# A hybrid conv and Fourier-mixer kernel: 25-point products, inverse and half of the mix in 64 by 64 parts of the array

## The chip, the cores and the metric

The kernel runs on one core of one Trainium2 chip. The time is that of the device in microseconds, from the first instruction to the last. A core has TensorE (a 128 by 128 array for matmuls, which writes PSUM), VectorE, ScalarE, GpSimd and SyncE (which here issues the DMAs). Each engine works through its own list of instructions in order and waits on semaphores for the others.

## The reference, cut to what matters

```python
B, R, C, H = 64, 55, 96, 192                      # 64 images, 55 x 55, 96 channels; 3025 tokens each
# layer 0: depthwise 25 x 25 convolution with every third tap, gate, residual
x = conv(x, raw_kernel * mask) * x + bias + x
# layer 1, t = tokens of x
h = relu(bn(layernorm(t) @ w1.T))                 # 3025 x 192
X = fft(h, axis=tokens, norm='ortho')
rd, idg = diagonal(r), diagonal(i)
xr = relu(X.real * rd - X.imag * idg + rb)
xi = relu(X.imag * rd + X.real * idg + ib)
y = ifft(xr + 1j * xi, axis=tokens, norm='ortho').real
t = t + bn(y @ w2.T)                              # back to 96 channels
t = t + ffn(layernorm(t))                         # 96 -> 384 -> 96, relu, inputs rounded to fp8
```

## The kernel before

It has two stages, one after the other: the convolution for all images (up to about 860 us), and the mixer for all images. Only the mixer is touched.

The mixer does the Fourier transform of 3025 = 121 x 25 points in two steps. First a product over the 121 rows (`rows`, 128 outputs: real and imaginary part of 62 row frequencies k1, in order [real/imaginary, kk, p] with k1 = 2p + kk). Its result goes to DRAM (`a_d`) and comes back (`acol`) with the 25 tokens on the partitions: 100 partitions are real/imaginary and kk times 25. Then, for each of 31 pairs p of row frequencies, the 25-point product with twiddles (`columns`, constants `fb`, 100 by 100). What is computed there for two values of kk does not mix, so half of each 100 by 100 constant is zero. The outputs have channels on the partitions, 96 at a time (`hf` is the half of the 192 channels), and stand in two PSUM banks (`COL`). The gate makes xr and xi of it: `gate_value` and the three operations of `gate_sum` on ScalarE, `value` (two operations), `larger` and `join` on VectorE, `cut_value` and `add_sum` on GpSimd. Then `mix` multiplies by w2 (two matmuls for each pair, one for each half of the channels, which accumulate), `out_mix` copies, `inverse` is the inverse 25-point product (100 by 100 again), `out_inverse` copies, the result goes through DRAM (`g_d`) into `grow`, and `inverse_rows` ends the transform. The feed-forward part follows: `normalise`, `turn2`, `up`, `out_up`, `widen_bias`, `down`, `out_down`, `finish`.

Everything is a software pipeline over 512 chunks, eight per image. In slot g of the schedule each engine runs one chunk of every stage, each at its own distance behind: GATE = 10 means that columns, gate_value and gate_sum of chunk g - 10 stand in slot g; MIX is 14, INV 15, ROWS 29, UP 41, DOWN 42. A chunk of the token stages is three tokens (of 25), the first of the eight is four. A chunk of the frequency stages is 8 pairs (7 in the last group) for one half of the channels; mix and inverse take four pairs (three in the last). The order within a slot is written out by hand, once for each engine: the four loops `for g in SLOTS_G` at the end of the engines' blocks. Buffers are few: most PSUM banks have one use per slot, so nearly every matmul group waits until the copy of the group before it in the same bank is done.

The lines that matter: the products L1033, widen L1045 (copy with relu L811), rows L1058 (copy L864), mix L1073 and L1074 (copy L819), inverse L1085 (copy L825), down L1097 (copy L833), turn L1110 (copy L841), up L1123 (copy L850), inverse rows L1134, turn2 L1145 (copy L780); the gate on ScalarE L789, L798, L801, L803. The second half of a chunk's rows is done in the next slot, `rows(g - 1, 1)`. The waits that the prediction follows: rows wait for relu of their own half, up for out_down of the chunk before (which stands in the same slot), mix for out_up of the slot before:

```python
            def rows(n, part):
                pe.wait_ge(hid_ready, 2 * n + part + 1)
            def up(n):
                pe.wait_ge(z_ready, n)
            def mix(n):
                    pe.wait_ge(y16_ready, upto(n + MIX - UP))
```

Of the kernel before, what the change touches and what calls it, by code (L numbers as in the profile page):

```python
# [84 lines left out]
SLOTS = PAIRS_K + 1  # L85
M = 4 * SLOTS
# [4 lines left out]
MIXED = (0, 4, 8, 12, 16, 20, 24, 28, 31)  # L91
# [30 lines left out]
def pairs_of(n):  # L122
    return MIXED[n % NS], MIXED[n % NS + 1]

# [6 lines left out]
def here(n):  # L131
    return 0 <= n < CHUNKS
# [6 lines left out]
def transform_constants():  # L139
# [15 lines left out]
    for kk in range(2):  # L155
        for p in range(PAIRS_K):
# [8 lines left out]
    out = {"c_fa": fa, "c_fb": fb.reshape(Q, PAIRS_K, Q), "c_ib": ib.reshape(Q, PAIRS_K, Q),  # L165
           "c_ia": np.ascontiguousarray(fa.T), "c_id": np.eye(128)}
# [180 lines left out]
def mixer_stage(nc, x1, p, a_d, g_d, out):  # L347
    with ExitStack() as ctx:
# [8 lines left out]
        fb = sb("fb", [Q, PAIRS_K, Q])  # L357
        ib = sb("ib", [Q, PAIRS_K, Q])
# [3 lines left out]
        w2t = sb("w2t", [HH + 1, 2, C])  # L362
        rd = sb("rd", [HH, 2])
        nrd = sb("nrd", [HH, 2])
        idg = sb("idg", [HH, 2])
        rb = sb("rb", [HH, 2])
        ibias = sb("ibias", [HH, 2])
# [11 lines left out]
        acol = sb("acol", [Q, PAIRS_K, H])  # L379
        spec = sb("spec", [HH + 1, 2, PAIRS_K, Q])  # L380
        gc = [sb(f"gc{s}", [HH, KC, Q // 2]) for s in range(2)]
        gq = [sb(f"gq{s}", [HH, KC, Q // 2]) for s in range(2)]
        gv = [sb(f"gv{s}", [HH, KC, Q // 2]) for s in range(2)]
        mixed = sb("mixed", [Q, SLOTS, C])
# [21 lines left out]
        with ExitStack() as wctx:  # L406
            def wsem(name):
# [4 lines left out]
            w2n = t_res[0:C, 2:4, :].rearrange("p a b -> p (a b)")  # L412
# [11 lines left out]
            rows = [spec[C:C + 1, 1, 2 * n:2 * n + 2, 0:C] for n in range(4)]  # L424
            rows2 = [spec[C:C + 1, 1, 8 + n, 0:C] for n in range(4)]
# [3 lines left out]
                      [spec[C:C + 1, 1, 12 + 2 * n:14 + 2 * n, 0:C] for n in range(2)],  # L429
                      [spec[C:C + 1, 1, 16 + n, 0:C] for n in range(2)]]  # L430
# [9 lines left out]
            LOADS = 30  # L440
# [3 lines left out]
            def _(sp):  # L444
# [4 lines left out]
                ld(ib[:, :, :], p["c_ib"])  # L449
# [3 lines left out]
                ld(w2n, p["w2"])  # L453
# [12 lines left out]
                ld(rb[:, :], p["rb"].rearrange("(a p) -> p a", a=2))  # L466
                ld(ibias[:, :], p["ib"].rearrange("(a p) -> p a", a=2))
                for dst, k in ((rd, "r"), (idg, "i")):
                    flat = p[k].rearrange("a b -> (a b)")
                    for a in range(2):  # L470
                        at = a * HH * (H + 1)
                        ld(dst[:, a:a + 1],
                           flat[at:at + (HH - 1) * (H + 1) + 1:H + 1].rearrange("(p o) -> p o", o=1))
# [739 lines left out]
```

## Time and profile before

| | us |
|---|---|
| median of 3 runs | 5028.19 |
| their range | 5025.69 to 5029.70 |
| the profiled execution | 5025.73 |
| its span in the trace | 5023.9 |
| mean granted TensorE clock | 0.964 |

Busy shares in the profile are times in which an engine had an instruction under way. A TensorE row with "x16" is 16 passes merged: it begins with the first start and ends with the last end. The ends of passes are modelled, and passes overlap, so what a stretch of passes costs is read from start to start. An f32 matmul shows as two passes, each with a weight load (PEld) of its own. Shapes of TensorE rows read: contraction rows * output partitions, then the moving operand. In the timeline the first number is the start in us, the second the duration, and brackets give the idle time just before and the instruction that ended it. The granted clock is a share of 2.4 GHz.

The page's slices:

```profile
PE   8999995599999999999999999999999999999964
DVE  3444443347888888888888888888888888888885
ACT  3444442278888888888888888888888888888853
PEclk9999997599999999999999999999999999999985
```

Each digit is a fortieth of the span, in tenths. The convolution is in the first seven, then comes the set-up of the mixer, and from the ninth on the mixer runs evenly until the last two.

### The profile page before, as it was taken

How to read it: one execution, taken by the hardware profiler on the slowest of the kernel's cores; microseconds unless marked ns; L12 is line 12 of the kernel's file. 1: busy time of each engine (PE TensorE's matmuls, PEld its weight loads, DVE VectorE, ACT ScalarE, POOL GpSimd, SP SyncE). 2: the span in 40 equal slices, each digit the busy share in tenths (PEclk: the TensorE clock that was granted, in tenths of full speed). 3: DMA queues.
4: the chain of work that ended last, by engine and by line, in shares of the span. 5: the costliest groups of instructions: out<-in, count | busy, mean ns of one | idle time of the engine just before them, and what ended most of it. 6: DMA issues, size and time to landing. Idle time of an engine off the chain costs nothing.

```text
span 5023.9 us, 121831 instructions
## 1 busy us (share of the span) xinstructions
PE 4688.8 (93%) x40863; PEld 4162.2 (83%) x40863; DVE 3875.6 (77%) x10873; ACT 3777.1 (75%) x7819; POOL 2493.3 (50%) x2603
## 2 busy tenths in 40 slices
PE   8999995599999999999999999999999999999964
PEld 7888884388888888888888888888888888888852
DVE  3444443347888888888888888888888888888885
ACT  3444442278888888888888888888888888888853
POOL 2334432144555555555555555555555555555542
PEclk9999997599999999999999999999999999999985
DMA  6777876256666666666666666666666666666541
GB/s 202 244 232 226 250 230 179 77 146 183 176 181 182 182 180 176 176 180 180 181 179 179 176 179 182 179 182 178 181 183 174 178 180 180 180 179 178 160 112 32
DMA packets 781424, 893.16 MB, mean 178 GB/s; under 512 B 236243, under 2 KB 689292, under 8 KB 768652
## 3 DMA queue, kind: packets, MB, share of 16 engines
q1 hardware_dynamic: 780556, 885.27, 63.9%
q8 instruction: 347, 5.69, 0.5%
q14 instruction: 257, 2.11, 0.1%
q10 hardware_dynamic: 264, 0.10, 0.0%
HBM read 500.64 MB, written 384.61 MB: 176 GB/s over the span
## 4 chain that ended last, share of the span: by engine, by line
PE 64%; DVE 13%; issue 3%; ACT 2%; DMA 0%; DVEq 0%; POOL 0%; POOLq 0%; ACTq 0%
PE ps L1033 10%; PE ps L1058 10%; PE ps L1045 9%; PE ps L1085 6%; PE ps L1074 6%; PE ps L1073 6%; PE ps L1134 5%; PE ps L1123 4%; PE ps L1097 4%; PE ps L1110 3%; DVE y L933 1%; PE ps L1145 1%; DVE bn L988 1%; DVE gv L958 1%; DVE xn L973 1%
## 5 line engine op out<-in xcount | busy, mean ns | idle before, releaser
L733 POOL TENSOR_SCALAR gv<-gv 96x400 f32<-96x400 f32 (+1 forms) x512 | 599.8, 1171 | 1615.4 <-DVE xn L973 1529.9
L1033 PE MATMUL ps<-fb,acol 100*96 100x100 f32 x7936 | 785.0, 252 | 44.0 <-DVE spec L965 43.6
L340 PE MATMUL cps<-toep,xin 114*128 114x190 f32 (+2 forms) x3456 | 777.2, 339 | 44.5 <-issue 25.4
L850 ACT ACTIVATE y<-ps 128x1089 f16<-128x1089 f32 (+1 forms) x512 | 573.0, 1119 | 315.9 <-PE ps L1123 315.9
L1058 PE MATMUL ps<-hid,fa 121*128 121x384 f32 (+1 forms) x2048 | 729.7, 438 | 46.7 <-DVE t L997 34.4
L1033 PEld LDWEIGHTS ps<-fb,acol 100*96 100x96 f32 x7936 | 722.1, 163 | 61.2 <-issue 60.8
L317 DVE SCALAR_TENSOR_TENSOR xo<-cps,xo 128x180 f32<-128x180 f32 (+3 forms) x576 | 362.8, 630 | 460.9 <-ACT xo L286 460.5
L286 ACT ACTIVATE xo<-cps 128x180 f32<-128x180 f32 (+3 forms) x576 | 367.4, 638 | 452.7 <-PE cps L343 452.7
L1045 PE MATMUL ps<-w1t,xnt 97*121 97x192 f32 x3200 | 701.2, 330 | 0.7 <-ACT xnt L841 0.7
L1073 PE MATMUL ps<-w2t,spec 97*100 97x96 f32 x3968 | 672.9, 251 | 4.7 <-ACT y L850 4.7
L1074 PE MATMUL ps<-w2t,spec 96*100 96x96 f32 x3968 | 675.6, 252 | 0.0
L933 DVE TENSOR_SCALAR y<-y,b1q 128x364 f16<-128x364 f16 (+1 forms) x1536 | 572.6, 427 | 98.7 <-ACT y L850 98.2
L340 PEld LDWEIGHTS cps<-toep,xin 114*128 114x128 f32 x3456 | 531.7, 194 | 108.8 <-issue 31.1
L295 POOL TENSOR_TENSOR xo<-xo,conv_cbias 128x3960 f32<-128x3960 f32 (+1 forms) x39 | 317.6, 8169 | 516.3 <-DVE xo L317 516.3
L939 DVE CAST hq<-y 128x1092 fp8e5<-128x1092 f16 (+1 forms) x512 | 517.5, 1011 | 53.8 <-DVE y L933 1.4
L1073 PEld LDWEIGHTS ps<-w2t,spec 97*100 97x100 f32 x3968 | 546.3, 167 | 5.2 <-POOL spec L739 2.7
L1085 PEld LDWEIGHTS ps<-mixed,ib 100*100 100x100 f32 x3968 | 430.8, 168 | 144.4 <-issue 78.5
L1045 PEld LDWEIGHTS ps<-w1t,xnt 97*121 97x121 f32 x3200 | 525.1, 187 | 19.0 <-issue 1.2
L1074 PEld LDWEIGHTS ps<-w2t,spec 96*100 96x100 f32 x3968 | 510.3, 168 | 0.0
L811 ACT ACTIVATE hid<-ps 121x384 f32<-121x384 f32 (+1 forms) x1024 | 432.7, 423 | 92.7 <-PE ps L1045 53.9
L739 POOL TENSOR_TENSOR spec<-spec,gc 96x400 f32<-96x400 f32 (+1 forms) x512 | 484.8, 947 | 0.0
L864 ACT ACTIVATE arow<-ps 128x384 f32<-128x384 f32 (+1 forms) x1024 | 426.5, 417 | 57.4 <-PE ps L1058 55.5
(107 smaller groups left out, 10243.1 us busy)
## 6 DMA issues: line engine op xcount, KB each, us to landing
a_d<-arow SPq DMA_DIRECT2D x448, 288.0 KB, 5.0
acol<-a_d SPq DMA_DIRECT2D x192, 600.0 KB
xin<-in_items SPq DMA_DIRECT2D x96, 1008.0 KB
g_d<-mixed SPq DMA_DIRECT2D x256, 300.0 KB
tok<-x_d SPq DMA_DIRECT2D x64, 1134.4 KB
out<-o_sb SPq DMA_DIRECT2D x448, 136.1 KB
x_d<-xo SPq DMA_DIRECT2D x48, 990.0 KB, 11.9
grow<-g_d SPq DMA_DIRECT2D x128, 312.0 KB, 11.1
```

The costliest lines, as they stand in the source:

```text
L340: last = nc.tensor.matmul(ps[2 * (m % DEEP)][:, (r0 - o0) * GC:(r1 - o0) * GC], xb, toep[e % 2][0:GP, c, at * GC:(at + r1 - r0) * GC], sta ...
L733: nc.gpsimd.tensor_scalar(v, v, 0.0, None, ALU.max).then_inc(v_cut, 1)
L739: nc.gpsimd.tensor_tensor(sv, sv, gc[t % 2][:, 0:n, :], ALU.add).then_inc(s_ready, 1)
L850: nc.scalar.activation(y16[n % 2][:, :, 0:w], ps[:, MIXP:MIXP + FM, 0:w], ACT.Copy).then_inc(y16_ready, 1)
L933: last = nc.vector.tensor_scalar(y[:, m, 0:w], y[:, m, 0:w], b1q[:, m:m + 1], 0.0, ALU.add, ALU.max)
L939: nc.vector.tensor_copy(q[:, :, 0:w], y[:, :, 0:w], saturate=False).then_inc(hq_ready, 1)
L1033: last = nc.tensor.matmul(COL[:, p, 0:Q], acol[:, p0 + p, hf * HH:(hf + 1) * HH], fb[:, p0 + p, :], start=True, stop=True)
L1045: last = nc.tensor.matmul(ps[0:U, WIDE, j * H:(j + 1) * H], xnt[n % 2][:, s0 - c0 + j, :], w1t[:, :], start=True, stop=True)
L1058: nc.tensor.matmul(ps[0:M, ROW, 0:(s1 - s0) * H], fa[:, :], hid[part][:, 0:s1 - s0, :].rearrange("p j h -> p (j h)"), start=True, stop=Tru ...
L1073: nc.tensor.matmul(o, spec[0:HH + 1, 0, p, :], w2t[0:HH + 1, 0, :], start=True, stop=False)
L1074: last = nc.tensor.matmul(o, spec[0:HH, 1, p, :], w2t[0:HH, 1, :], start=False, stop=True)
L1085: last = nc.tensor.matmul(ps[0:Q, INVP, (p - p0) * C:(p - p0 + 1) * C], ib[:, p, :], mixed[:, p, :], start=True, stop=True)
```

## The change

K2 is 50, HALF 64, S 25, C 96, QG 8. The constants, their tiles and the gate's tiles take another shape, the products, the inverse and half of the mix become matmuls with at most 64 rows and 64 columns, and the order within a slot changes on TensorE, ScalarE and VectorE.

- `columns`: the zero half of each constant is dropped. kk (now r) has the partitions 64r to 64r + 49 of `acol` and `fb`, and its 50 by 50 products go to bank r. The channels are cut in 128 and 64 instead of 96 and 96. In a slot with hf = 0 there are 8 pairs x 2 r x 2 blocks of 64 channels = 32 matmuls, in one with hf = 1 16, whose outputs alternate between the lower and the upper 64 partitions. Each has 64 output rows and 50 columns. Consecutive matmuls go round the four quarters of the array.
- The gate works on 128 partitions: 400 elements for hf = 0, 200 for hf = 1 (before 400, or 350 in the last group, in both).
- `mix`: for the first 128 channels one whole-array matmul per tile of two row frequencies (114 output partitions), then for the last 64 channels two matmuls of 64 rows and 50 outputs each, which accumulate onto it. The bias of the second batch norm becomes a matmul of its own in the first chunk of an image (before, a row of ones in `spec`).
- `inverse`: 8 matmuls of 50 rows and 64 outputs instead of 4 of 100 by 100. Mix and inverse share two PSUM banks now, so `inverse` waits for the `out_mix` of the chunk that stands in the same slot.
- Order: on TensorE the products move behind the mix and the inverse directly behind them, ahead of rows(g, 0). On ScalarE out_mix comes behind relu(g, 0), then gate_value, the copy of rows(g, 0), out_inverse, and only then gate_sum. On VectorE value and larger move from the end of the slot to the next slot, behind residual.
- The column loads and the mixed stores are issued in two halves each. The rows of `c_ia` are in another order to match.

```diff
@@ tiles @@
-        fb = sb("fb", [Q, PAIRS_K, Q])
-        ib = sb("ib", [Q, PAIRS_K, Q])
+        fb = sb("fb", [128, SLOTS, K2])
+        ib = sb("ib", [128, 2, TILES, HALF])
-        acol = sb("acol", [Q, PAIRS_K, H])
-        spec = sb("spec", [HH + 1, 2, PAIRS_K, Q])
+        acol = sb("acol", [128, PAIRS_K, H])
+        spec = [sb("spec0", [128, 4, 2 * QG, HALF]), sb("spec1", [128, 4, QG, HALF])]
-        TURNED, WIDE, ROW, MIXP, INVP, DOWNP = 2, 3, 4, 5, 6, 7
+        TURNED, WIDE, ROW, MIXP, DOWNP = 2, 3, 4, 5, 7
@@ TensorE, columns @@
-                for p in range(n):
-                    last = nc.tensor.matmul(COL[:, p, 0:Q], acol[:, p0 + p, hf * HH:(hf + 1) * HH],
-                                            fb[:, p0 + p, :], start=True, stop=True)
+                for k in range(QG):
+                    l, j = (k, 0) if hf == 0 else (k // 4 * 4 + k % 2 * 2 + k // 2 % 2, k % 2)
...
+                    for r in range(2):
+                        for h in range(2 - hf):
+                            at = HALF * (h + j)
...
+                            last = nc.tensor.matmul(ps[at:at + HALF, r, c0:c0 + K2],
+                                                    acol[HALF * r:HALF * r + K2, p, HALF * (h + 2 * hf):HALF * (h + 2 * hf) + HALF],
+                                                    fb[HALF * r:HALF * r + K2, p, :], start=True, stop=True)
@@ TensorE, mix @@
-                for p in range(p0, p1):
-                    o = ps[0:Q, MIXP, (p - p0) * C:(p - p0 + 1) * C]
-                    nc.tensor.matmul(o, spec[0:HH + 1, 0, p, :], w2t[0:HH + 1, 0, :], start=True, stop=False)
-                    last = nc.tensor.matmul(o, spec[0:HH, 1, p, :], w2t[0:HH, 1, :], start=False, stop=True)
+                for a in range(tiles):
+                    at = (QG * r + 2 * a) * HALF
+                    nc.tensor.matmul(ps[0:HALF + K2, MIXP + a % 2, MIXC + a // 2 * C:MIXC + (a // 2 + 1) * C],
+                                     wide[:, at:at + HALF + K2], w2t[:, 0, :],
+                                     start=(a < 2), stop=False, skip_group_check=True)
...
+                for a in range(tiles):
+                    j = a % 2
+                    for b in range(2):
+                        last = nc.tensor.matmul(ps[HALF * b:HALF * b + K2, MIXP + j, MIXC + a // 2 * C:MIXC + (a // 2 + 1) * C],
+                                                spec[1][HALF * j:HALF * j + HALF, q, QG // 2 * r + a // 2 * 2 + b, 0:K2],
+                                                w2t[HALF * j:HALF * j + HALF, 1, :],
+                                                start=False, stop=True, skip_group_check=True)
@@ TensorE, inverse @@
-                pe.wait_ge(w2_ready, n + 1)
+                pe.wait_ge(w2_ready, upto(n + 2))
...
-                    last = nc.tensor.matmul(ps[0:Q, INVP, (p - p0) * C:(p - p0 + 1) * C], ib[:, p, :],
-                                            mixed[:, p, :], start=True, stop=True)
+                    for b in range(2):
+                        last = nc.tensor.matmul(ps[HALF * j:HALF * j + HALF, MIXP + b, INVC + a // 2 * C:INVC + (a // 2 + 1) * C],
+                                                ib[HALF * b:HALF * b + K2, r, 4 * q + a, :],
+                                                mixed[HALF * b:HALF * b + K2, QG * q + 4 * r + a, :],
+                                                start=True, stop=True, skip_group_check=True)
@@ VectorE, slot @@
                 if here(g - RES):
                     residual(g - RES)
+                if here(g - GATE - 1):
+                    value(g - GATE - 1)
+                    larger(g - GATE - 1)
...
-                if here(g - GATE):
-                    value(g - GATE)
-                    larger(g - GATE)
```

ScalarE, one slot of the kernel before, from gate_value (`gq`) on; `spec`, `gc` and the write to `ps` are gate_sum:

```order
L789 ACTIVATE gq1<-ps,ibias,idg 96x400
L864 ACTIVATE arow2<-ps 128x192
L811 ACTIVATE hid0<-ps 121x384
L798 ACTIVATE spec<-ps,idg 96x8x50
L801 ACTIVATE gc1<-ps,rb,rd 96x400
L803 ACTIVATE ps<-ps,rb,rd 96x8x50
L819 ACTIVATE mixed<-ps 100x384
L864 ACTIVATE arow0<-ps 128x384
L825 ACTIVATE mixed<-ps 100x384
L833 ACTIVATE z161<-ps 121x288
L841 ACTIVATE xnt0<-ps 97x484
L811 ACTIVATE hid1<-ps 121x192
```

ScalarE, the same stretch in the changed kernel; `mixed` is out_mix first and out_inverse second:

```order
L900 ACTIVATE arow0<-ps 128x192
L840 ACTIVATE hid0<-ps 121x384
L856 ACTIVATE mixed<-ps 114x2x2x96
L819 ACTIVATE gq0<-ps,ibias,idg 128x400
L900 ACTIVATE arow1<-ps 128x384
L861 ACTIVATE mixed<-ps 114x2x2x96
L827 ACTIVATE spec0<-ps,idg 128x16x25
L830 ACTIVATE gc0<-ps,rb,rd 128x400
L832 ACTIVATE ps<-ps,rb,rd 128x16x25
L869 ACTIVATE z160<-ps 121x288
L877 ACTIVATE xnt1<-ps 97x363
L840 ACTIVATE hid1<-ps 121x384
```

The gate's last three operations stood ahead of the copies of mix, rows and inverse and now stand behind them; gq follows out_mix.

TensorE, the kernel before, from rows(g, 0) of one slot to the first products of the mix in the next:

```order
L1058 MATMUL ps<-hid,fa 128x384
L1085 MATMUL ps<-mixed,ib 100x96 x4
L1097 MATMUL ps<-w2q,hq 128x96 x9
L1110 MATMUL ps<-ident,toks 97x121 x4
L1045 MATMUL ps<-w1t,xnt 121x192
L1134 MATMUL ps<-grow,ia 121x288
L1123 MATMUL ps<-xq,w1q 128x363 x3
L1145 MATMUL ps<-ident,xn 96x121 x3
L1033 MATMUL ps<-fb,acol 96x100 x7
L1058 MATMUL ps<-hid,fa 128x192
L1045 MATMUL ps<-w1t,xnt 121x192 x2
L1073 MATMUL ps<-w2t,spec 100x96
```

TensorE, the changed kernel, from rows(g - 1, 1) to turn2, one slot:

```order
L1102 MATMUL ps<-hid,fa 128x192
L1089 MATMUL ps<-w1t,xnt 121x192 x2
L1121 MATMUL ps<-w2t,spec 114x96 x4
L1130 MATMUL ps<-w2t,spec 50x96 x8
L1076 MATMUL ps<-fb,acol 64x50 x32
L1146 MATMUL ps<-mixed,ib 64x96 x8
L1102 MATMUL ps<-hid,fa 128x384
L1160 MATMUL ps<-w2q,hq 128x96 x12
L1173 MATMUL ps<-ident,toks 97x121 x3
L1089 MATMUL ps<-w1t,xnt 121x192
L1197 MATMUL ps<-grow,ia 121x288
L1186 MATMUL ps<-xq,w1q 128x363 x3
```

The products (`fb,acol`) led the slot, ahead of the rows with 192 columns; now they stand behind both kinds of mix, and the inverse (`mixed,ib`) ahead of the rows with 384 columns. The second listing has three kinds of small matmul in a row and whole ones before and after.

## Rows read from the trace of the kernel before

**Rows 1.** page, first part: busy us, share of the span and passes of each engine
```profile
PE 4688.8 (93%) x40863; PEld 4162.2 (83%) x40863; DVE 3875.6 (77%) x10873; ACT 3777.1 (75%) x7819; POOL 2493.3 (50%) x2603
```

**Rows 2.** groups of instructions, 2000 to 4000 us: line, engine, tiles, shapes, count, busy, mean
```profile
L1033 PE MATMUL ps<-fb,acol 100*96 100x100 f32 x4092 | 403.1, 251 | 14.7 <-DVE spec L965 14.7
```

**Rows 3.** timeline of TensorE, a plain slot: start us, us, line, tiles, shapes, count
```profile
3034.14 1.57 PE L1033 MATMUL ps<-fb,acol 100*96 100x100 f32 x16
3035.54 0.52 PE L1058 MATMUL ps<-hid,fa 121*128 121x192 f32 x2
3035.89 0.81 PE L1045 MATMUL ps<-w1t,xnt 97*121 97x192 f32 x4
3036.55 0.33 PE L1073 MATMUL ps<-w2t,spec 97*100 97x96 f32 x2
...
3037.95 0.84 PE L1058 MATMUL ps<-hid,fa 121*128 121x384 f32 x2
...
3040.88 0.63 PE L1123 MATMUL ps<-xq,w1q 96*128 96x363 fp8e5 x3
3041.35 0.33 PE L1145 MATMUL ps<-ident,xn 121*96 121x121 fp8e5 x3
3041.51 0.71 PE L1033 MATMUL ps<-fb,acol 100*96 100x100 f32 x6
```

**Rows 4.** timeline of ScalarE, the next slot; in brackets the idle time before
```profile
3044.50 0.58 ACT L798 ACTIVATE spec<-ps,idg 96x400 f32<-96x400 f32 x1
3044.98 0.68 ACT L801 ACTIVATE gc<-ps,rb,rd 96x400 f32<-96x400 f32 x1
3045.55 0.65 ACT L803 ACTIVATE ps<-ps,rb,rd 96x400 f32<-96x400 f32 x1
...
3046.41 0.49 ACT L864 ACTIVATE arow<-ps 128x384 f32<-128x384 f32 x1
3046.78 0.50 ACT L825 ACTIVATE mixed<-ps 100x384 f32<-100x384 f32 x1
3047.15 0.43 ACT L833 ACTIVATE z<-ps 121x288 f16<-121x288 f32 x1
3047.44 0.50 ACT L841 ACTIVATE xnt<-ps 97x363 f32<-97x363 f32 x1
3047.79 0.36 ACT L811 ACTIVATE hid<-ps 121x192 f32<-121x192 f32 x1
3048.72 1.08 ACT L850 ACTIVATE y<-ps 128x1089 f16<-128x1089 f32 x1 [0.57 <-PE ps L1123]
```

**Rows 5.** set-up: busy by stretch (granted clock third last), the line's durations, timeline
```profile
860.00:900.00 40.00, 2.18 (x31) 1.80 (x31) 19.00 (x58) 0.83 (x4) 0.00 (x0) 0.50 0.17 37
...
L575 PE MATMUL ps<-ident,stage x24: 311/311/367, 888.4 to 889.0; 64*64 64x64 f32 x24
...
887.73 0.69 PE L570 MATMUL ps<-ident,t_res 96*128 96x96 f32 x3
...
888.05 0.37 PE L570 MATMUL ps<-ident,t_res 96*128 96x96 f32 x1
888.35 0.38 PE L575 MATMUL ps<-ident,stage 64*64 64x64 f32 x4
...
888.35 0.49 PE L575 MATMUL ps<-ident,stage 64*64 64x64 f32 x8
```

**Rows 6.** timeline of TensorE while the mixer fills, rows behind a wait
```profile
995.05 0.91 PE L1058 MATMUL ps<-hid,fa 121*128 121x384 f32 x2 [0.58 <-ACT hid L811]
```

**Rows 7.** timeline of TensorE while the mixer fills, two slots on
```profile
1039.40 1.58 PE L1033 MATMUL ps<-fb,acol 100*96 100x100 f32 x16 [0.24 <-DVE spec L965]
...
1045.94 1.58 PE L1033 MATMUL ps<-fb,acol 100*96 100x100 f32 x16 [0.53 <-DVE spec L965]
```

**Rows 8.** busy time by stretch: TensorE, loads, VectorE, ScalarE, GpSimd, clock, DMA
```profile
3000.00:4000.00 1000.00, 983.96 (x9181) 885.07 (x9180) 895.33 (x2619) 874.90 (x1861) 558.55 (x660) 1.00 0.67 179
4808.00:4820.00 12.00, 8.40 (x87) 6.85 (x85) 11.45 (x33) 6.75 (x12) 6.30 (x7) 1.00 0.14 39
```

More of the change, by code:

```diff
@@ L85 @@
 SLOTS = PAIRS_K + 1
+K2 = 2 * S
+HALF = 64
+TILES = SLOTS // 2
+QG = 8
 M = 4 * SLOTS
@@ L378, in mixer_stage @@
         arow = [sb(f"arow{s}", [M, JC, H]) for s in range(AR)]
-        acol = sb("acol", [Q, PAIRS_K, H])
-        spec = sb("spec", [HH + 1, 2, PAIRS_K, Q])
[L381 to L384, printed above, removed]
+        acol = sb("acol", [128, PAIRS_K, H])
+        spec = [sb("spec0", [128, 4, 2 * QG, HALF]), sb("spec1", [128, 4, QG, HALF])]
+        gc = [sb(f"gc{s}", [128, 2 * QG, S]) for s in range(2)]
+        gq = [sb(f"gq{s}", [128, 2 * QG, S]) for s in range(2)]
+        gv = [sb(f"gv{s}", [128, 2 * QG, S]) for s in range(2)]
+        mixed = sb("mixed", [128, SLOTS, C])
         grow = sb("grow", [M, S, C])
@@ L542, in _ @@
                 nc.vector.tensor_copy(ident8[:, :], ident[0:U, 0:U], saturate=False)
-                nc.vector.memset(mixed[:, PAIRS_K, :], 0.0)
+                for v in spec:
+                    nc.vector.memset(v[:, :, :, K2:HALF], 0.0)
                 for v in toks:
@@ L549, in _ @@
                     nc.vector.memset(v[:, :, :], 0.0)
-                then(nc.vector.memset(spec[HH:HH + 1, :, :, :], 0.0))
-                nc.vector.memset(spec[HH:HH + 1, 0, 0, 0:1], 1.0)
             @block.scalar
@@ L675, in store_mixed @@
                 sp.wait_ge(g_ready, n + 1)
-                p0, p1 = GROUP[q], GROUP[q + 1] if q < 3 else SLOTS
-                sp.dma_start(g_d[i].rearrange("s (r p) c -> (s r) p c", p=SLOTS)[:, p0:p1, :],
-                             mixed[:, p0:p1, :]).then_inc(g_stored[q], 16)
+                dst = g_d[i].rearrange("s (ri j p) c -> j (s ri) p c", ri=2, j=2)
+                for j in range(2):
+                    sp.dma_start(dst[j, :, QG * q:QG * (q + 1), :],
+                                 mixed[j * HALF:j * HALF + K2, QG * q:QG * (q + 1), :]).then_inc(g_stored[q], 16)
             def load_back(i, h):
@@ L784, in gate_value @@
             def gate_value(t):
-                n, hf = group(t)[2:]
+                _, hf, n = group(t)
                 act.wait_ge(x_done, t + 1)
@@ L875, in _ @@
                     relu(g, 0)
+                if here(g - MIX):
+                    out_mix(g - MIX)
+                if here(g - GATE):
+                    gate_value(g - GATE)
+                if here(g):
+                    rows_out(g, 0)
+                if here(g - INV):
+                    out_inverse(g - INV)
                 if here(g - GATE):
@@ L948, in value @@
             def value(t):
-                p0, p1, n, hf = group(t)
-                xi = COL[:, 0:n, Q // 2:Q]
-                dv = spec[0:HH, hf, p0:p1, Q // 2:Q]
+                _, hf, n = group(t)
+                xi, dv = column(t, 1), spectrum(t, 1)
                 dve.wait_ge(c_ready, t + 1)
@@ new lines, in mix @@
+                for a in range(tiles):
[3 more added lines that the diff above has]
+                                     start=(a < 2), stop=False, skip_group_check=True)
+                if n % NS == 0:
+                    nc.tensor.matmul(ps[0:HALF + K2, MIXP, MIXC:MIXC + C], hot[:, :], wb[:, :],
+                                     start=False, stop=False, skip_group_check=True)
@@ L1157, in _ @@
                     mix(g - MIX)
+                if here(g - GATE):
+                    columns(g - GATE)
+                if here(g - INV):
+                    inverse(g - INV)
                 if here(g):
                     rows(g, 0)
-                if here(g - INV):
-                    inverse(g - INV)
                 if here(g - DOWN):
```

162 lines of the change are left out of this document (91 added, 71 removed).

## The prediction

> **What bounds the kernel now.** I began with the busy shares. TensorE is busy for 93% of the span, VectorE 77%, ScalarE 75% [rows 1]. The slices show a convolution stage up to about 860 us and then the mixer, in which nothing changes until 4840 us; the change touches only the mixer. There the mean slot of the schedule comes from the grouped view: 4092 passes of the 25-point products in 2000 us, and a batch of eight slots has 124 of them, so 33.0 batches, 60.6 us each, **7.58 us a slot** [rows 2]. The timeline of a plain slot (three tokens, 16 product passes) is 7.37 us of TensorE without a hole, from 3034.14 to 3041.51 [rows 3]. ScalarE has the same period and waits 0.57 us in it for the up-projection [rows 4]. So TensorE is the bound, and work taken from it should show, as long as no chain of waits across engines becomes longer than its work.
>
> An f32 matmul is two passes. With 96 to 100 columns on either side, loads and streams overlap and a pass costs 0.088 us: 16 products take 1.40 us (3034.14 to 3035.54), 16 of the mix 1.40 us, so 8 of the inverse 0.70 us. Two passes of rows with 192 columns take 0.35 us [rows 3]. I read from this 2 cycles a column of the wider side at 2.4 GHz and some 5 to 15 ns; a whole pass of 114 columns is then 0.10 us.
>
> **What the parts cost.** The trace has one burst of the kind that the change uses: 24 passes of 64 by 64 in the set-up, going round the four quarters. The clock is 0.50 there, 1.2 GHz [rows 5]. A merged row runs from its first start to its last end, and a pass shows 0.311 us (the first ones 0.367): four passes have begun by about 888.37, eight by 888.53, and the last of 24 begins at 889.0 [rows 5]. So behind the second group come four groups in about 0.45 us, 0.11 us each. That is one pass's own 128 cycles of 1.2 GHz, so four run at once, 27 ns a pass. At 2.4 GHz I take four per pass time of the wider side: 0.058 us for 64 columns (14.5 ns each), 0.085 us for 96 (21 ns each). This is an extrapolation; it is held at 27 ns below for the upper bound. Entering the parts is not free: the last whole pass before the burst began at 888.05 and the first small one at 888.35, where whole ones followed at 0.16 us, and the second small group ends its starts 0.16 us after the first and not 0.11: 0.19 us more in all, at half clock [rows 5]. No row has the way back at full clock. I bound a change of form by nothing and 0.3 us, and take 0.15 us, twice a slot.
>
> The Trainium skill's TensorEngine Tiling (Key Properties) says that a change of tiling mode drains TensorE. The 0.30 us gap agrees. By that rule two drains per slot are due, by a free switch none.
>
> TensorE's work per slot, before and after, in us. Products: 1.40 becomes 64 passes in a slot with the first 128 channels ("wide"), 0.93, and 32 in one with the last 64 ("narrow"), 0.46. Mix: 16 passes, 1.40, become 8 whole ones at 0.10 and 16 small ones at 0.021, 1.14. Inverse: 0.70 becomes 16 at 0.021, 0.34. With two switches: 3.50 becomes 2.71 or 2.24. TensorE alone would fall by about 1 us per slot, to some 6.5 us. ScalarE and VectorE lose something too: a narrow gate has 200 elements instead of 400, and ScalarE's copies of 288 and 384 elements (0.29 and 0.37 us) [rows 4] show 0.8 ns an element, so 0.17 us an operation, four on each.
>
> **The wait that the order makes.** The change moves the products behind the mix and, on ScalarE, the gate's three operations behind the two copies that wait for work after the products. Follow it round: rows(g-1, 1) may begin only when relu(g-1, 1) is done, the last but one thing that ScalarE does in its slot. Then TensorE does rows, widen, mix, products, inverse and rows(g, 0); ScalarE copies the result of rows(g, 0), copies the inverse, does the gate's three, out_down, out_turn and relu(g, 1); and only then the next slot's second rows can begin. Also up(g-41) waits for out_down of the same slot. Before, the same ring was some 5.4 us (0.35, 0.65, 1.40, 0.67 and 0.87 to the inverse's end, then copies and relu of 1.4 us), because the gate stood before the copy of rows(g, 0) and the products before rows(g-1, 1). Now nearly everything is in it. Clock it from the start of rows(g-1, 1), wide slot:
>
> - rows 0.35, and 0.07 since its load can't be made ahead (0.91 us behind a wait, 0.84 us without) [rows 3, 6]; widen 0.65: 1.07. The mix also waits for out_up of the slot before: that up begins 0.63 us ahead of our zero, its last pass ends 0.63 us after its start, hand-over 0.04, out_up 1.08, hand-over 0.05: 1.18. With 0.07 for the load: 1.25.
> - whole mix 0.80: 2.05. Switch 0.15, small mix 0.34: 2.54. Products 0.93: 3.47. Inverse 0.34, switch 0.15: 3.96. rows(g, 0) 0.84 to its end [rows 3]: 4.80.
> - ScalarE [rows 4]: 0.04, arow 0.37, inverse 0.37: 5.58. Gate 0.48, 0.57, 0.57: 7.20. out_down 0.43: 7.63.
> - up 0.05 later, 0.47, and 0.16 for turn2: **8.31**. The other branch (z 0.29, xnt 0.35, relu 0.36, 0.05) gives 8.25.
>
> Narrow slot: the products are done before out_mix. Small mix ends at 2.54 + 0.17 of tail, 0.04, out_mix 0.49, 0.05: 3.29; inverse 3.63; rows(g, 0) ends at 4.62; copies 5.40; gate 1.11: 6.51; out_down, up and turn2: **7.62**. The mean is 7.96. In a batch one slot has the four-token rows (0.3), one the four-token out_up (0.3), with 0.1 in small copies; the last mix has three tiles (-0.4); the root adds 0.13: together +0.06 per slot. So **8.02 us against 7.58, +0.44 us** in the 470 slots in which all stages run: +207 us. In the 28 slots of the fill that have products and mix, but no down or up, a slot takes 6.54 us now [rows 7]; the ring without out_down and up is 7.8 or 7.1: +0.9 us, +25 us. Seven more small loads and a memset in the set-up: some 5 us. Sum on the profiled execution, whose span is 5023.9 us (its own time is 5025.7, the median of the runs 5028.2): **5260 us**.
>
> Edits that I cost at nothing: VectorE's value and larger now follow residual; the products wait for them, but residual ends before rows(g-1, 1) begins and 1.65 us of work is done well before 2.54. They push the cast that down waits for back by 1.65 us; down now starts later in the slot as well. If that cover is gone, turn and widen follow late, off the ring, up to about a microsecond. The two halves of each column load and of each mixed store carry the same bytes on SP, with one more issue each, two slots ahead of use. The bias matmul (two passes a batch) is 0.2 us.
>
> **Rivals.**
> - Small passes have a floor. If no more than one pass per 27 ns can be issued also at full clock (the rate of the burst), small mix and inverse are 0.43 each and products 1.71 or 0.85: +0.96 us wide, +0.28 us narrow, +0.62 us mean: 5570 us. For it: no row shows a faster sustained rate. Against it: within a group starts are 5 to 7 ns apart, and 27 ns is just what the half clock gives. The Trainium skill's TensorE: Matmul & The Clock Gate (on the 56 ns gap) has a floor of 25 ns from start to start; the starts within the burst do not obey it, and its sustained form would give this rival.
> - Faster than before. If queued passes start as closely as within a group of the burst (6 ns) and a switch costs nothing, 64 passes cost 0.4 us and the mix's small part 0.1. The ring then falls to 7.3 and 6.8, with the extras 7.1, and the time to 5025.7 - 0.48 x 470, 4800 us. It decides once the mean slot of 8.02 falls by 0.44 us: switches (0.30) and the two exposed loads with what hangs on them (0.2) hold that much and no more, so small passes must be cheaper than I take them as well. With switches and loads free alone the mean is 7.5 and the kernel stays where it is.
> - Clock. TensorE would be at work 80% of the time. 87 passes in 12 us still had clock 1.00, where a full stretch has 9181 in 1000 us, 110 in 12 [rows 8]. Were quarters of the array not to hold it, a slot at 1.2 GHz costs 3.5 us more, 1600 us in all.
> - The parts do not overlap: each pass 0.058 or 0.085 us, +3.3 us a slot. The burst speaks against it.
>
> **How the numbers follow.** Forecast 0.60: switches between 0 and 0.3 us and loads exposed or not give 5030 to 5400 us, likeliest 5260. Floor 0.18: 5400 to 5580 us. Faster 0.13: 4800 to 5010 us. No change 0.05. Clock or no overlap 0.04. The range 5030 to 5590 us takes in the first two and part of the fourth, 0.8. About 0.2% is what a measurement of this kernel can tell from no change. Faster 0.13, within it 0.05, slower 0.82.
>
> **What will show it.** Right: TensorE busy clearly below 93%; in each slot a wait of 1 us or more ahead of the up-projection for ScalarE's z, and ScalarE waiting for mix and for rows(g, 0), 1 to 1.5 us a slot, where its one long wait was for up; wide slots 0.6 to 0.7 us longer than narrow ones; products 0.93 us for 64 passes. Wrong: TensorE without holes and a slot below 7.4 us (ring misread), products of 1.7 us (floor), clock below 1.00 in the mixer, or whole passes following small ones without a gap.

## The result and the profile after

| | before | changed |
|---|---|---|
| median, us | 5026.9 | 5622.8 |
| range of the runs | 5009.3 to 5029.7 | 5609.6 to 5650.8 |
| ratio, with its 95% interval | | 1.120 (1.115 to 1.125) |
| span of the profiled execution | 5023.9 | 5613.3 |

The changed kernel is 12% slower, 596 us. The forecast was 5260 us, slower by 4.6%, with a range up to 5590: the direction was right, the size was not, and the time lies outside the range.

The page of the changed kernel, busy shares and slices, answers to [rows 1]:

```profile
PE 4597.5 (82%) x64799; PEld 3680.2 (66%) x64799; DVE 3488.5 (62%) x10875; ACT 3668.6 (65%) x7819; POOL 2282.0 (41%) x2603
...
PE   8999985788888888888888888888888888888864
...
PEclk9999995889999999999999999999999999999965
```

All engines are busy for less of the span than before, TensorE 82% instead of 93%, and no other has taken its place. That is the picture of a chain of waits, not of an engine at its limit. The groups of instructions from 2000 to 5000 us (line, shapes, count, then busy us, mean ns, then idle us before them and who ended it):

```profile
L1076 PE MATMUL ps<-fb,acol 50*64 50x50 f32 x15996 | 310.7, 221 | 1.0 <-issue 1.0
...
L1146 PE MATMUL ps<-mixed,ib 50*64 50x96 f32 x5332 | 194.9, 259 | 22.6 <-ACT mixed L856 17.7
L1186 PE MATMUL ps<-xq,w1q 96*128 96x363 fp8e5 x903 | 188.8, 317 | 360.8 <-ACT z L869 359.9 <-issue 0.5
```

A batch has 124 passes of the inverse, so 5332 in 3000 us are 43.0 batches of 69.8 us: **8.72 us a slot**, against 7.58 [rows 2] and 8.02 forecast. 1.14 us more in the 470 full slots is 536 us of the 596. The idle time stands where it was forecast, before `up`, ended by ScalarE's z. TensorE's timeline from the rows of one slot to those of the next, a wide slot with narrow rows around it (answers to [rows 3]):

```profile
3029.70 0.56 PE L1102 MATMUL ps<-hid,fa 121*128 121x192 f32 x2
3030.10 0.81 PE L1089 MATMUL ps<-w1t,xnt 97*121 97x192 f32 x4
3030.88 1.01 PE L1121 MATMUL ps<-w2t,spec 128*114 128x96 f32 x8
3031.82 0.55 PE L1130 MATMUL ps<-w2t,spec 64*50 64x96 f32 x16
3032.19 0.98 PE L1076 MATMUL ps<-fb,acol 50*64 50x50 f32 x56
3033.00 0.55 PE L1146 MATMUL ps<-mixed,ib 50*64 50x96 f32 x16
3033.47 0.91 PE L1102 MATMUL ps<-hid,fa 121*128 121x384 f32 x2
...
3037.49 0.62 PE L1186 MATMUL ps<-xq,w1q 96*128 96x363 fp8e5 x3 [1.22 <-ACT z L869]
3037.95 0.38 PE L1208 MATMUL ps<-ident,xn 121*96 121x121 fp8e5 x4
3038.16 0.87 PE L1102 MATMUL ps<-hid,fa 121*128 121x384 f32 x2
```

ScalarE's in the same slot (answers to [rows 4]); brackets give idle time and who ended it:

```profile
3032.44 0.49 ACT L856 ACTIVATE mixed<-ps 114x384 f32<-114x384 f32 x1 [0.75 <-PE ps L1130]
3033.24 0.68 ACT L819 ACTIVATE gq<-ps,ibias,idg 128x400 f32<-128x400 f32 x1 [0.31 <-PE ps L1076]
3034.42 0.49 ACT L900 ACTIVATE arow<-ps 128x384 f32<-128x384 f32 x1 [0.50 <-PE ps L1102]
3034.81 0.48 ACT L861 ACTIVATE mixed<-ps 114x384 f32<-114x384 f32 x1
3035.18 0.62 ACT L827 ACTIVATE spec<-ps,idg 128x400 f32<-128x400 f32 x1
3035.66 0.69 ACT L830 ACTIVATE gc<-ps,rb,rd 128x400 f32<-128x400 f32 x1
3036.23 0.68 ACT L832 ACTIVATE ps<-ps,rb,rd 128x400 f32<-128x400 f32 x1
3036.80 0.44 ACT L869 ACTIVATE z<-ps 121x288 f16<-121x288 f32 x1
```

Read the two together from 3029.70. The parts do on TensorE what they should. ScalarE stands idle three times, 1.56 us in all, because TensorE has not come so far; behind 3034.42 it works without a hole up to z, and TensorE waits 1.22 us for z. Each waits for the other in turn, and nothing of the saved work is left over.

One more thing happens, once a batch, and with it, in most batches, a fall of the clock. VectorE, TensorE and the granted clock (third from last in the row by stretch), all from the changed kernel:

```profile
3016.43 0.47 DVE L956 RECIPROCAL diff<-rstd 121x50 f32<-121x50 f32 x1 [2.12 <-ACT rstd L892]
...
3018.11 0.46 DVE L1031 TENSOR_TENSOR t<-ps,t_res 121x288 f32<-121x288 f32 x1 [0.24 <-DVE rstd L960]
...
3016.95 0.62 PE L1186 MATMUL ps<-xq,w1q 96*128 96x363 fp8e5 x3 [1.68 <-ACT z L869]
...
3018.71 0.98 PE L1102 MATMUL ps<-hid,fa 121*128 121x192 f32 x2 [0.98 <-DVE t L1031]
...
3018.00:3028.00 10.00, 9.29 (x94) 8.13 (x95) 5.32 (x16) 4.43 (x11) 4.99 (x6) 0.51 0.54 138
```

`root`, one small ScalarE instruction per image, stands behind the gate, and the gate is now late. So VectorE waits 2.1 us for it, its residual (`t`) comes late, and TensorE waits a second time, right after the wait for z. About there the clock falls to 1.2 GHz for ten microseconds; from the rows at 3018.71 to the inverse rows TensorE needs 9.69 us, where the narrow slot from 3038.16 needs 5.70. This slot lasts from 3016.95 to 3029.00, 12.05 us, where the other narrow slots from 2930 to 3050 us take 7.74 to 8.06. It is the longest of its kind from 2000 to 4000 us: the slot with the late root takes 8.84 us where the clock stays at 1.00, and 10.1 us in the mean.

### The profile page after: what moved, and what is told of

Its sections match the earlier page's. It is cut to its first block, busy times and chain, and to the rows that moved or that the text cites. A ratio compares the mean times of both kernels' runs of the same rounds, so it can differ in the third digit from the quotient of the medians.

```text
span 5613.3 us, 170250 instructions
## 1 busy us (share of the span) xinstructions
PE 4597.5 (82%) x64799; PEld 3680.2 (66%) x64799; DVE 3488.5 (62%) x10875; ACT 3668.6 (65%) x7819; POOL 2282.0 (41%) x2603
## 4 chain that ended last, share of the span: by engine, by line
PE 40%; issue 20%; ACT 14%; POOL 7%; DVE 2%; DMA 0%; ACTq 0%; POOLq 0%; DVEq 0%
PE ps L1102 10%; PE ps L1121 7%; PE ps L1089 5%; PE ps L1186 4%; PE ps L1076 4%; PE ps L1130 4%; ACT ps L832 4%; PE ps L1146 3%; ACT spec L827 2%; ACT gc L830 2%; ACT z L869 2%; POOL gv L763 2%; ACT y L886 2%; POOL z L775 2%; POOL spec L769 1%
## 5 line engine op out<-in xcount | busy, mean ns | idle before, releaser
L763 POOL TENSOR_SCALAR gv<-gv 128x400 f32<-128x400 f32 (+1 forms) x512 | 488.4, 954 | 2006.7 <-DVE xn L1007 1846.8
L1031 DVE TENSOR_TENSOR t<-ps,t_res 121x288 f32<-121x288 f32 (+1 forms) x512 | 240.7, 470 | 1036.1 <-PE ps L1197 1020.3
L1186 PE MATMUL ps<-xq,w1q 96*128 96x363 fp8e5 (+1 forms) x1536 | 345.9, 335 | 576.2 <-ACT z L869 574.6
L1186 PEld LDWEIGHTS ps<-xq,w1q 96*128 96x128 fp8e5 x1536 | 119.3, 98 | 842.6 <-issue 808.2
L1121 PEld LDWEIGHTS ps<-w2t,spec 128*114 128x114 f32 x3968 | 494.5, 196 | 150.4 <-issue 149.4
L1121 PE MATMUL ps<-w2t,spec 128*114 128x96 f32 x3968 | 542.0, 283 | 54.5 <-ACT y L886 36.0
L775 POOL TENSOR_TENSOR z<-z,b2q 121x288 f16<-121x288 f16 (+1 forms) x512 | 384.7, 751 | 475.7 <-ACT z L869 475.5
L856 ACT ACTIVATE mixed<-ps 114x384 f32<-114x384 f32 x512 | 251.1, 490 | 449.6 <-PE ps L1130 449.6
L969 DVE TENSOR_SCALAR y<-y,b1q 128x364 f16<-128x364 f16 (+1 forms) x1536 | 396.5, 315 | 130.2 <-ACT y L886 129.6
L789 POOL TENSOR_TENSOR toks<-tok,rstd 121x288 f32<-121x288 f32 (+1 forms) x512 | 353.8, 691 | 295.2 <-DVEq L961 250.4
```

Of the source, the lines that this page charges most:

```text
L763: nc.gpsimd.tensor_scalar(v, v, 0.0, None, ALU.max).then_inc(v_cut, 1)
L775: nc.gpsimd.tensor_tensor(z, z, b2[:, 0:c1 - c0, :], ALU.add).then_inc(z_biased, 1)
L969: last = nc.vector.tensor_scalar(y[:, m, 0:w], y[:, m, 0:w], b1q[:, m:m + 1], 0.0, ALU.add, ALU.max)
L1121: nc.tensor.matmul(ps[0:HALF + K2, MIXP + a % 2, MIXC + a // 2 * C:MIXC + (a // 2 + 1) * C], wide[:, at:at + HALF + K2], w2t[:, 0, :], sta ...
L1186: last = nc.tensor.matmul(ps[:, MIXP + m, 0:w], w1q[:, m * 128:(m + 1) * 128], xq[n % XR][:, 0:w], start=True, stop=True)
```

## The experiments

Theory A: the ring (rows, mix, products, inverse, rows, two copies, gate, z, up; z is what out_down writes) sets the slot, and the late root, the clock and a slow hand-over to `up` make up what the forecast lacked. Rival B: the small parts and the changes of form on the array are what costs. The ten variants were timed beside the kernel before on the same chip (its median there 5022 to 5023 us; 5027 us beside the changed kernel). A difference between two rows is one of medians: the executions of a kernel spread by 8 to 22 us, those of the changed kernel by 41 and of the filler before up by 58.

| kernel | us | ratio to before |
|---|---|---|
| changed | 5623 | 1.120 (1.115 to 1.125) |
| root early | 5489 | 1.094 (1.091 to 1.097) |
| gate and root early | 5103 | 1.016 (1.014 to 1.019) |
| root, then gate early | 5097 | 1.015 (1.013 to 1.017) |
| order of before, small parts | 4986 | 0.993 (0.991 to 0.996) |
| the same, inverse behind down | **4898** | **0.975 (0.973 to 0.977)** |
| z's wait last | 5561 | 1.107 (1.105 to 1.109) |
| root early and z's wait last | 5412 | 1.078 (1.077 to 1.080) |
| filler before rows | 5547 | 1.105 (1.102 to 1.107) |
| filler before up | 5514, 5523, 5572, and one of 11200 | 1.105 (1.098 to 1.111) |
| down behind widen | 5310 | 1.057 (1.054 to 1.060) |

### Root early

```diff
                 if here(g - GATE):
                     gate_value(g - GATE)
+                if g % NS == 6 and 0 <= (g + 2) // NS < B + 5:
+                    root((g + 2) // NS)
                 if here(g):
                     rows_out(g, 0)
...
                     gate_sum(g - GATE)
-                if g % NS == 6 and 0 <= (g + 2) // NS < B + 5:
-                    root((g + 2) // NS)
```

> The changed kernel with one ScalarE instruction moved: root (once an image) goes from behind the gate's last operations to ahead of the copy of rows(g, 0). Theory A: once a batch VectorE waits 2.1 us for root, residual comes late, TensorE waits 0.98 us before the rows, and with the up wait of 1.68 us just before it the clock falls to 0.50 for some 9 us; these slots of 10.5 to 12 us become 7.8 us. That is 3 to 4 us a batch, so 5370 to 5430 us, and the clock in the mixer 1.00. Rival B (the small parts and the switches of the array are what costs): the move changes nothing that can be measured beyond 1 us a batch, 5560 us or more.

5489 us, 134 us less: 2.1 us a batch, not the 3 to 4 expected. Rival B is hit (it allowed 1 us a batch), but A overrated it. The late residual is gone: no wait of the rows for VectorE's `t` is left from 2000 to 4000 us, where the changed kernel has 29. The clock is not mended: stretches below full clock from 2000 to 4000 us come to 61 us at half clock, where the changed kernel has 142 us (summed over stretches of 1 us). In this kernel's trace it also falls behind the gap before `up` alone; TensorE and the stretch behind:

```profile
3009.93 0.62 PE L1186 MATMUL ps<-xq,w1q 96*128 96x363 fp8e5 x3 [1.54 <-ACT z L869]
...
3012.00:3014.00 2.00, 2.00 (x28) 1.83 (x32) 1.90 (x8) 0.62 (x3) 0.00 (x0) 0.50 0.40 123
```

The slot behind takes 9.91 us. Most slots with the same gap keep their clock.

### Gate early, and root ahead of it

```diff
                 if here(g - GATE):
                     gate_value(g - GATE)
+                if here(g - GATE):
+                    gate_sum(g - GATE)
+                if g % NS == 6 and 0 <= (g + 2) // NS < B + 5:
+                    root((g + 2) // NS)
                 if here(g):
                     rows_out(g, 0)
...
-                if here(g - GATE):
-                    gate_sum(g - GATE)
-                if g % NS == 6 and 0 <= (g + 2) // NS < B + 5:
-                    root((g + 2) // NS)
```

> The changed kernel with gate_sum and root moved on ScalarE to directly behind gate_value, ahead of the copy of rows(g, 0); nothing else. Theory A (a ring from rows through the gate to the next rows sets the slot): the gate then runs while TensorE does inverse and rows(g, 0); wide slots fall from 8.5 to about 7.9 us, narrow ones from 7.8 to about 6.8, and the late root is gone too; 4970 us, between 4900 and 5080. Rival B (small parts and switches cost the time): at least 5400 us.

5103 us: the gate's three operations and root at another place in the same slot take back 520 of the 596 us, 386 of them beyond root early, with every small part as it was. That decides between A and B. It did not reach the 4970 us expected, nor the 5080 that were the upper end. In its trace the ring is no longer the only bound. TensorE in a wide slot, and ScalarE:

```profile
3009.47 0.49 PE L1089 MATMUL ps<-w1t,xnt 97*121 97x192 f32 x2
3010.58 0.72 PE L1197 MATMUL ps<-grow,ia 128*121 128x288 f32 x2 [0.62 <-issue]
...
3009.98 0.50 ACT L900 ACTIVATE arow<-ps 128x384 f32<-128x384 f32 x1
```

The inverse rows use the bank of rows(g, 0) and start 0.10 us behind the end of its copy (3010.48), which now stands behind the gate; the profile names no releaser, the wait stands in the code. And `down` waits for VectorE's cast, the load of its first pass 79.5 us in 2000 us (the view of waits):

```profile
PEld ps L1160 <- DVE hq L975: 79.5, 94, 1.8
```

That is the cover I named for value and larger ahead of the cast, and here it is gone: 0.3 us a slot on the loads, of which 0.13 us (33.2 us in 2000) is idle time of the matmuls themselves. Not all of it is due to VectorE's new order, since the fastest kernel below has VectorE's old order and still 41.4 us of this wait on the loads.

The next kernel has root ahead of gate_value instead, and is otherwise the same.

> As the kernel with gate_sum and root directly behind gate_value, but root ahead of gate_value. Theory A: there VectorE already gets root in time, so the time is within 15 us of that kernel's 5103 us. If the once-a-batch lateness of residual is still on the path, 5040 us or less.

5097 us, as theory A had it: root is in time either way.

### The order of before with the small parts

```diff
@@ TensorE @@
+                if here(g - GATE):
+                    columns(g - GATE)
                 if here(g - 1):
                     rows(g - 1, 1)
...
-                if here(g - GATE):
-                    columns(g - GATE)
-                if here(g - INV):
-                    inverse(g - INV)
                 if here(g):
                     rows(g, 0)
+                if here(g - INV):
+                    inverse(g - INV)
```

ScalarE's order and the place of value and larger go back too.

> The changed kernel with the order of before on TensorE, ScalarE and VectorE: products at the head of the slot, inverse behind rows(g, 0), gate ahead of the copies. The small parts stay, but stand in three separate places, so there are six changes of form a slot instead of two. Theory A: ring is short again, TensorE's work is 6.2 us and six switches of 0.1 us, and the inverse waits some 0.5 us for the mix copy of its own slot: about 7.2 us a slot, 4870 us (4780 to 5000). Rival B: the small parts cost, with six switches more than with two: above 5620 us.

4986 us, faster than before by 0.7%, with six changes of form a slot instead of two. Rival B asked for more than 5620 us and falls. The time lies in the range that I gave (4780 to 5000) and misses the 4870 us, for a reason that the trace shows:

```profile
3005.33 0.91 PE L1102 MATMUL ps<-hid,fa 121*128 121x384 f32 x2
3006.74 0.56 PE L1146 MATMUL ps<-mixed,ib 50*64 50x96 f32 x16 [0.49 <-ACT mixed L856]
```

The inverse may not write into the shared banks before the mix of its own slot is copied out, and here that comes late: 1.41 us from rows to inverse, where the rows cost 0.75. The next kernel puts down's 0.4 us in there:

```diff
-                if here(g - INV):
-                    inverse(g - INV)
                 if here(g - DOWN):
                     down(g - DOWN)
+                if here(g - INV):
+                    inverse(g - INV)
```

out_inverse goes behind out_down as well.

> As the kernel with small parts and the order of before (4986 us), but inverse behind down on TensorE, and out_inverse behind out_down on ScalarE. There the inverse waits 1.1 us a slot in all for the mix copy of its own slot (load and matmul rows), because mix and inverse share banks. Theory A: down's 0.4 us goes into that wait; a slot falls by 0.3 to 0.4 us, 4800 to 4870 us. Rival (six switches and TensorE's work are its bound): no change, 4980 us.

4898 us, 2.5% faster than before and the fastest of the study; 89 us gained, where 120 to 190 us were expected. TensorE in its trace, wide slot and beginning of the next:

```profile
3000.26 1.15 PE L1076 MATMUL ps<-fb,acol 50*64 50x50 f32 x64
3001.34 0.59 PE L1102 MATMUL ps<-hid,fa 121*128 121x192 f32 x2
...
3003.30 0.55 PE L1130 MATMUL ps<-w2t,spec 64*50 64x96 f32 x16
3003.78 0.91 PE L1102 MATMUL ps<-hid,fa 121*128 121x384 f32 x2
3004.53 0.68 PE L1160 MATMUL ps<-w2q,hq 128*128 128x96 fp8e5 x12
3005.18 0.56 PE L1146 MATMUL ps<-mixed,ib 50*64 50x96 f32 x16
```

There is no wait of ScalarE's making left in these slots (16.6 us in 2000 us, on the loads of the inverse). It also prices the change of form: the products with whole passes on both sides take 1.08 us where they take 0.92 between other small ones, the small mix 0.48 instead of 0.37. That is the way back to the whole array. The way in shows between the last whole pass of a mix and the first small one, 0.19 us from start to start where whole ones follow at 0.10. About 0.1 us for each change.

### The hand-over to up

```diff
                 if n:
-                    pe.wait_ge(z_ready, n)
                     pe.wait_ge(y16_ready, n)
+                    pe.wait_ge(z_ready, n)
```

> The changed kernel with two waits of up swapped on TensorE, so that the wait for out_down (z) is the last one before the matmuls. In the changed kernel up begins 0.25 us behind the end of out_down, where 0.05 us was forecast. Theory A: the sequencer passes the waits behind z only once z is there, so the hand-over shrinks by 0.05 to 0.1 us a slot and the time by 25 to 50 us, 5570 to 5600 us. Rival: the 0.25 us is the restart of TensorE's queue behind any explicit wait, and nothing changes (within 0.3%).

5561 us, 62 us less, more than the 25 to 50 expected. The gap between the end of z and the start of `up` shrank from 0.25 us (3037.24 to 3037.49 above) to 0.15 us. ScalarE and TensorE of this kernel:

```profile
3002.69 0.43 ACT L869 ACTIVATE z<-ps 121x288 f16<-121x288 f32 x1
...
3003.27 0.62 PE L1186 MATMUL ps<-xq,w1q 96*128 96x363 fp8e5 x3 [1.57 <-ACT z L869]
```

0.10 us in 512 slots is 51 us. The traces agree: batches with the clock at 1.00 throughout take 67.0 us here and 67.8 us in the changed kernel. So in `up` a wait that stands behind the one that blocks costs time on its own, though its condition has long been true. It is not a price of every such wait: the inverse has two waits behind the one for `mixed` and starts 0.05 us after it ends, in all of its 98 waits from 2000 to 4000 us. Why these two differ is open.

> The changed kernel with both small repairs, root ahead of the copy of rows(g, 0) and the wait for z last in up. Each alone took 134 and 62 us off. If the once-a-batch stall and the hand-over are two separate terms, they add: 5420 to 5440 us. If both are the same time seen twice (the clock's), the sum is nearer to 5480 us.

5412 us, 211 us below the changed kernel, where the two apart give 134 and 62. The two add up to 196 us, and the 15 us more are within the spread of the executions, so the once-a-batch stall and the hand-over are two terms.

### The clock

Two kernels fill idle time of TensorE with matmuls that nobody reads. The first moves nothing else, the second has z's wait last as well.

```diff
+                if g % NS == 7 and here(g - ROWS - 1) and here(g - 1):
+                    pe.wait_ge(hid_ready, 2 * g)
+                    for _ in range(5):
+                        nc.tensor.matmul(ps[0:M, WIDE, 384:512], fa[:, :], fa[:, :], start=True, stop=True)
                 if here(g - 1):
                     rows(g - 1, 1)
```

> The changed kernel with five whole f32 matmuls of 128 columns (1.1 us, their output isn't used) ahead of rows(g-1, 1) in the slot where TensorE waits 0.98 us for residual, once a batch. They take away the idle time there, not the lateness of residual. Theory A with the clock as its larger part: the clock stays at 1.00, the slot after falls from 10.5 to 12 us to about 8.7, so 2 to 3 us a batch, 5430 to 5500 us. If the lateness of residual is the whole of it and the clock costs little: within 15 us of the changed kernel, or slower by up to 70 us where the filler is longer than the wait.

```diff
@@ TensorE, up @@
                 if n:
-                    pe.wait_ge(z_ready, n)
                     pe.wait_ge(y16_ready, n)
+                for _ in range(4):
+                    nc.tensor.matmul(ps[0:M, MIXP, 0:128], fa[:, :], fa[:, :], start=True, stop=True)
+                if n:
+                    pe.wait_ge(z_ready, n)
```

> The changed kernel with four whole f32 matmuls of 128 columns (0.9 us, output not used) ahead of up in every slot, in the time in which TensorE waits 0.9 to 1.7 us for out_down. They do no useful work; they only fill that idle time. Theory A (the clock falls to 0.50 about once a batch, for 3.4 or 6.8 us, because of these gaps, and costs about 2 us each time): clock 1.00 in the mixer and 90 us less, 5500 to 5550 us. Rival (the half clock only marks time that is lost anyway): same time as the changed kernel, or slower by what the filler adds in short gaps.

The first takes 5547 us, 76 us less, though it adds work; the second 5514, 5523 and 5572 us. The time at half clock between 2000 and 4000 us falls from 142 us to 34 and 31. The first kernel came out 1.2 us a batch better, where 2 to 3 were expected: the residual stayed late. In the second one z's wait stands last, which alone is worth 62 us, so its filler can claim some 40 us of the 100 by which its middle time is less, and the first is the cleaner evidence. In 2000 us (28.6 batches) the first kernel has 108 us less at half clock and gains 1.2 us a batch, 34 us: a microsecond at half clock cost about a third of a microsecond, since part of it falls on time that is waited out anyway. The fourth execution of the second kernel took 11200 us, at a mean granted clock of 0.43 where the others have 0.95; no trace of it exists, and what it was is open.

The changed kernel's own trace prices the clock whole. Two batches that follow on each other, from one four-token `up` to the next:

```profile
2906.89:2974.60 67.71, 55.58 (x931) 43.57 (x932) 48.63 (x160) 51.25 (x115) 30.61 (x41) 1.00 0.60 162
2974.60:3045.55 70.95, 59.95 (x932) 47.48 (x932) 48.23 (x160) 51.28 (x115) 30.63 (x41) 0.93 0.57 154
```

Of the 47 batches from 1500 to 4800 us, 11 keep clock 1.00 and take 67.8 us in the mean, within 0.1 us; all together take 69.7 us. So the falls cost 1.9 us a batch, and the first filler took back 1.4 of them (68.3 us in its trace).

### Down behind widen

```diff
@@ TensorE, and the same for out_down behind relu(g, 1) on ScalarE; on top of root and gate early @@
-                if here(g - DOWN):
-                    down(g - DOWN)
                 if here(g - TURN):
                     turn(g - TURN)
                 if here(g):
                     widen(g, 1)
+                if here(g - DOWN):
+                    down(g - DOWN)
```

> As the kernel with root and gate ahead of the copy of rows(g, 0) (5097 us), with down behind turn and widen(g, 1) on TensorE and out_down behind relu(g, 1) on ScalarE. Two changes of form a slot. Theory C: what keeps that kernel above before is VectorE's order (value and larger ahead of the cast), for which down waits 0.3 to 0.5 us a slot; moved back by 0.7 us, down finds it ready and the slot falls by 0.3 us: 4930 to 4990 us. Rival: the ring through rows, gate, relu is still the bound there; then the time stays within 30 us of 5097 us, or rises, since out_down comes later for up.

5310 us, 212 us worse than its base: neither 4930 nor unchanged. The wait for the cast did vanish from the view of waits, but `up` waits for z, which came later, 147.9 us in 2000 us where the base had 5.9:

```profile
PE ps L1186 <- ACT z L869: 147.9, 244, 1.0
```

I had named that danger and underrated it. What VectorE's new order is worth by itself isn't settled by this kernel.

## Why the prediction was right and wrong

**The bound before, and what the parts cost: right.** Products take 0.92 us for 64 passes (0.93 forecast), 14.4 ns a pass, the median of 86 wide slots from 2000 to 4000 us whose passes are all in the trace; one of them:

```profile
3011.44 1.10 PE L1076 MATMUL ps<-fb,acol 50*64 50x50 f32 x64
3012.36 0.52 PE L1146 MATMUL ps<-mixed,ib 50*64 50x96 f32 x12
```

The small mix takes 0.37 us (0.34), the whole mix with the change of form behind it 0.94 us (0.95). So four parts run at once at full clock as they did at half, and the rivals of a floor at 27 ns and of no overlap fall. A change of form is 0.1 us, not 0.15.

**The ring: right, to 2% in the wide slot shown.** Offsets from the start of the rows, in the wide slot shown:

| | forecast | trace |
|---|---|---|
| whole mix begins | 1.25 | 1.18 |
| products begin | 2.54 | 2.49 |
| rows(g, 0) end | 4.80 | 4.68 |
| gate's last three begin | 5.58 | 5.48 |
| z ends | 7.63 | 7.54 |
| up begins | 7.68 | 7.79 |
| next rows | 8.31 | 8.46 |

The narrow slot came out at 7.74 to 8.06 us (7.62 forecast), without the one that has the late root. The experiment that takes the gate out of the ring gives back 520 us, root included.

**The hand-over to up: too small.** I took 0.05 us between the engines, as at the rows with one wait [rows 6]. `up` has five. It took 0.25 us; 0.2 us in the 470 full slots are 94 us, of which swapping two waits recovered 62, a part of that by fewer falls of the clock.

**The root: a step left out.** I added 0.13 us for the instruction itself and did not ask who waits for it, though I moved it with the gate by 1.5 us or more and VectorE's residual stands behind it. Root early recovers 134 us, 2.1 us a batch in its trace (67.6 instead of 69.7 us). Where the clock stays at 1.00 the batch falls by 0.9 us (66.8 instead of 67.8), nearly all of it in the one slot, from 8.84 to 7.99 us. So 0.9 is the stall and 1.2 the clock.

**The clock: a rival given too little.** It had its share of 0.04 with a price for a mixer wholly at half clock, and from the ramp-down stretch at clock 1.00 [rows 8] I gave it little chance. "Clock below 1.00 in the mixer" stood among my signs of being wrong, and it came. The truth lay between: the clock falls for 3.4 to 10.2 us about once a batch, 26 times from 2000 to 4000 us. Of these falls 22 stand within 2.6 us behind the start of an `up` that had waited 1.5 us or more; 83 of the 230 had. My sum had nothing for this, and it came to 1.9 us a batch, some 110 us in the 470 slots. The filler before rows took back 76.

**The rest.** The forecast lacked 0.70 us a slot, 5.6 us a batch (69.7 against 64.2). 1.9 are the clock, 1.6 the hand-over, 0.9 the late root. The rest, some 1.1 us a batch, is not assigned by an experiment. The trace has two candidates that I priced low: the slot with four-token out_up took 9.1 us against 8.6 forecast, and the bias matmul 0.29 us against 0.2, in the ring. So the mechanism was right, and the steps that failed are these three terms, one sized too small (the hand-over, 0.05 us taken and 0.25 measured), one held at nothing (the clock, 1.9 us a batch) and one with its waiters left out (root, 0.13 us taken and 0.9 more measured).

**The edits costed at nothing.** value and larger ahead of the cast cost nothing that can be seen in the changed kernel, for the ring gave `down` its cover; with the ring shortened `down` waits for the cast by up to 0.3 us a slot. What of this is their own cost no run separates. The column loads and mixed stores in two halves show no wait on the path.

## What to carry over

Before work is taken from the engine that bounds a pipeline, follow once round each loop through the engines that returns to the same instruction, with the new order: if the longest takes more time than the work that is left, the saving is lost and the order has to be found first. In a hand-written order look for instructions that come once in many slots (a root, a bias): they move with their neighbours, and their waiters are elsewhere. And a saving should be tried in the old order first; here it was worth 2.5% in an order close to the old one, with six changes of form a slot where the new order has two.

## What the hardware showed

- Four 64 by 64 parts work at the same time on f32 passes also at full clock: 14.4 ns a pass of 64 columns, sustained over 64 passes. Ahead of the run I had seen it only at half clock (27 ns).
- A change between whole array and parts costs about 0.1 us, in either direction: in, 0.19 us from start to start instead of 0.10; back, the small mix 0.48 us instead of 0.37.
- The clock fell to 1.2 GHz in the middle of a stretch in which TensorE was busy for 83% of the time, most often behind a gap of 1.5 to 1.9 us, with or without a second one of 1.0 us, and not behind every such gap. In the kernel before there is no such place from 2000 to 4000 us.
- In `up` a wait on TensorE that is already met still cost 0.10 us when it stood behind the one that blocks; at the inverse two such waits left the hand-over at 0.05 us.
